# A new order for the instructions of a fused Mamba and mixture-of-experts kernel, in the same four slots

## What is computed

```
x = x + 0.5 * ffn(layernorm(x))      # 8 experts 128 -> 512 -> 128, the top 2 weighted
h = layernorm(x)
x1 = h + mamba(rmsnorm(h))           # in_proj, conv of 4 taps, silu, x_proj, dt_proj, softplus,
                                     #   a scan over t with 16 states, gate, out_proj
m  = mamba(rmsnorm(x1))
x = x + x1 + memory_attend(m)        # m + 0.1 * (masked m m^T v) W_read
x = x + 0.5 * ffn(layernorm(x))
```

## Time and profile before

| | |
|---|---|
| median of 3 runs | 1785.68 us (1783.99 to 1789.38) |
| the profiled execution | 1783.98 us, of which the span 1782.2 us |
| VectorE | 1580.4 us busy, 89% of the span |
| TensorE | 1455.7 us busy, 82% |
| ScalarE | 1102.2 us busy, 62% |
| GpSimd | 300.9 us busy, 17% |
| DMA | 131.93 MB, mostly the 224 additions of `G` into `acc` |
| tensor clock, mean | 0.908 of 2.4 GHz |

### The profile page before, as it was taken

The page is one execution under the profiler, slowest core; times in us unless marked ns, Lnnn a source line. Parts: engine busy times, 40 slices in busy tenths (PEclk is TensorE's granted clock), DMA queues, the critical chain, the costliest instruction groups (busy, mean ns, idle before and its releaser), DMA issues. The chain is left out here.

```text
span 1782.2 us, 26252 instructions
## 1 busy us (share of the span) xinstructions
PE 1455.7 (82%) x8672; PEld 1251.2 (70%) x8672; DVE 1580.4 (89%) x2421; ACT 1102.2 (62%) x2173; POOL 300.9 (17%) x366
## 2 busy tenths in 40 slices
PE   5878656888989888988989888988989888568768
PEld 4767545777778777777878677776878677357757
DVE  5259999999999999999999999999999999999821
ACT  2267455756767666756766667756776677447422
POOL 0001121122112211122112221122112121121100
PEclk9989767999999899998999899998999899669869
DMA  5014344443443334433443334433344344443400
GB/s 200 1 23 79 76 80 82 89 83 60 78 85 73 66 73 88 89 72 60 82 86 72 72 72 90 85 75 61 73 79 80 63 81 89 83 83 72 93 8 7
DMA packets 43947, 131.93 MB, mean 74 GB/s; under 512 B 3984, under 2 KB 12176, under 8 KB 43664
## 3 DMA queue, kind: packets, MB, share of 16 engines
q0 software_dynamic: 32256, 117.45, 34.7%
q1 hardware_dynamic: 11536, 12.56, 2.2%
HBM read 10.46 MB, written 2.10 MB: 7 GB/s over the span
## 5 line engine op out<-in xcount | busy, mean ns | idle before, releaser
L927 DVE TENSOR_TENSOR_SCAN hs<-dA,dbu 128x1024 f32<-128x1024 f32 x256 | 583.8, 2286 | 5.2 <-issue 3.6
L575 ACT ACTIVATE raw<-b_h 128x512 f32<-128x512 f32 x512 | 305.7, 598 | 323.1 <-PE b_h L327 308.6
L636 ACT ACTIVATE dA<-delta,A 128x255 f32<-128x255 f32 x1024 | 421.7, 495 | 13.2 <-DVE delta L900 6.8
L1118 POOL DMA_DIRECT2D acc<-G x224 | 195.5, 873 | 1101.2 <-DVE G L939 658.0
L404 PE MATMUL b_r<-bcr,selr 128*128 128x256 f32 x1024 | 240.2, 330 | 134.2 <-DVE G L939 74.3
L917 DVE TENSOR_TENSOR dbu<-du,b_r 128x1024 f32<-128x1024 f32 x256 | 306.0, 1206 | 5.4 <-issue 3.6
L325 PE MATMUL b_h<-xh,w1h 128*128 128x512 f32 x512 | 245.5, 479 | 78.0 <-DVE ob L853 31.3
L404 PEld LDWEIGHTS b_r<-bcr,selr 128*128 128x128 f32 x1024 | 174.8, 203 | 175.2 <-DVE G L939 82.2
L939 DVE TENSOR_TENSOR G<-hs,b_r 128x1024 f32<-128x1024 f32 x224 | 271.9, 1214 | 8.2 <-issue 5.4
L334 PE MATMUL b_out<-w2s,raw 128*128 128x128 f32 x2048 | 252.3, 275 | 0.0
L334 PE MATMUL b_h<-w2s,raw 128*128 128x128 f32 x2048 | 250.2, 275 | 0.0
(11 more groups left out here) (137 smaller groups left out, 1408.2 us busy)
## 6 DMA issues: line engine op xcount, KB each, us to landing
acc<-G POOLq DMA_DIRECT2D x224, 512.0 KB, 4.5
xin<-x_dram SPq DMA_DIRECT2D x8, 256.0 KB, 2.8
raw<-w_dram SPq DMA_DIRECT2D x1, 2048.0 KB, 11.0
out_dram<-ob SPq DMA_DIRECT2D x8, 256.0 KB, 2.8
prm<-pack_dram SPq DMA_DIRECT2D x1, 1124.5 KB, 5.2
hs<-sel_dram SPq DMA_DIRECT2D x2, 512.0 KB, 12.3
G<-sel_dram SPq DMA_DIRECT2D x2, 512.0 KB, 7.5
dA<-early_dram SPq DMA_DIRECT2D x1, 512.0 KB, 11.4
```

Of the source, the lines that this page charges most:

```text
L575: do(hT[e % 2][:, c, :], H[i % 2][:, :], ACT.Silu).then_inc(f_hact, 1)
L636: last = do(dA[j % 4][:, d, k, 1:], delta[b][:, k, 1:], ACT.Exp, scale=A[:, k, s:s + 1])
L927: V.tensor_tensor_scan(flat(hs[j % 2]), flat(dA[j % 4]), flat(dbu[j % 2]), 0.0, ALU.mult, ALU.add)\
L1118: Q.dma_start(acc[b][:, :, :, :].rearrange("p d h t -> p (d h t)"), G[j % NG][:, :, :, :].rearrange("p d h t -> p (d h t)"), accum_op=ALU. ...
```

## The change: what it does

`ORDER` is written anew for all four slots on all four engines. The helpers, their instructions, operands, buffers and waits stay; no word moves to another slot. The numbers behind `p` change too, so that the experts' pieces stand elsewhere between the spreads. Two texts of the table (slot 2) as they were and as they are:

```diff
 "vector":
-        "flow b0 flog b1 s0 g0 gate s1 ftop xsum b2 g1 un lx s2 b3 g2 fweights s3 f0 b4 b5 ln g3 s4 f1 b6 g4 low "
-        "s5 s6 g5 b7 unx g6 s7 delta g7",
+        "b0 flow s0 flog ftop b1 g0 b2 gate s1 xsum g1 b3 fweights un s2 s3 g2 lx f0 b4 g3 s4 b5 f1 g4 ln low s5 "
+        "b6 b7 g5 unx s6 s7 g6 g7 delta",
```

More of the change, by code:

```diff
@@ L46 @@
     "tensor": (
[8 rows of a table removed]
+        "t0 t1 t2 fturn in fgate t3 p1 t4 t5 p8 t6 p1 xp t7 t8 p4 dt p3 t9 m1 t10 t11 p5 t12 m2 t13 p1 t14 p2 t15 "
+        "m3 m4 p3",
+        "t0 p2 t1 p1 t2 p1 t3 p4 t4 p2 t5 p2 out p4 t6 t7 p3 turn t8 p2 t9 in t10 p1 t11 p4 t12 p4 t13 p1 t14 p2 "
+        "xp t15 p1 dt p2",
+        "t0 fturn t1 fgate p1 t2 t3 p4 t4 p1 t5 out p3 t6 p4 turn t7 t8 in t9 p3 t10 xp t11 p3 t12 p2 t13 p2 dt "
+        "p1 t14 p2 t15 p5",
+        "t0 t1 turng t2 p2 in t3 p2 t4 p5 t5 p1 t6 p2 t7 xp t8 p3 t9 p1 t10 dt m1 p2 m2 t11 p2 t12 p2 t13 p7 t14 "
+        "p2 m3 t15 p2 m4",
     ),
     "scalar": (
[4 rows of a table removed]
[4 rows of a table added]
     ),
     "vector": (
[1 row of a table removed]
[1 row of a table added]
         "g5 s6 b7 g6 s7 xb g7",
[6 rows of a table removed]
[6 rows of a table added]
     ),
```

## The result

| | before | after |
|---|---|---|
| median of the runs | 1785.68 us | 1797.04 us (5 runs, 1795.43 to 1799.98) |
| ratio, 95% interval | | 1.0068 [1.0056, 1.008] |
| span of the profiled execution | 1782.2 us | 1795.2 us |
| mean tensor clock | 0.908 | 0.904 |
| VectorE, from its first scan product to the start of its last `gate` | 1584.3 us | 1600.6 us |

The last two rows are worked out from VectorE's timeline and its busy time: 111.14 to 1695.44 us and 109.37 to 1710.00 us for the first, 111.14 to 1689.18 and 109.37 to 1704.20 for the second, which is the prediction's 53.7 us but for its ends. The 16.3 us that the long part grew are the loss; the set-up ahead of it was 1.8 us shorter and the end 1.5 us, and 16.3 - 1.8 - 1.5 is the 13.0 us of the span. These are of one execution each.

A forecast was written before the change was run, and what follows sets the result against it. VectorE was taken to set the pace, with 53.7 us not busy. Gains of 17.5 us less new waits of 2.1 and 1.4 made 14.0, so 1783.98 became 1770.0, a median of 1771.7 us; 8-in-10 range 1763 to 1789.

The forecast's parts named there:

- Slot 2's logits: Slot 2: a scan as cover ends VectorE's wait on TensorE's logits; 6.9 us gained, nearly all waits on logits.
- `gate`: Slots 0, 1 and 2: `gate` stands behind two or more further words, so its 2.1 us of waits go.
- `xsum`: VectorE's three waits on `xsum` for `out`, 2.3 us, taken as gone, with a reserve for new waits.
- the 1.4 taken: Slot 2's `xsum`: less cover, margin 0.6 us; new waits of 0.2 us in 7 groups, bad case 15 us.
- the third tight place: Slot 0's `mask` waits for `m2`, now behind 22 pieces and not 18; taken as 0, upper bound 9 us.
- 17.5 - 1.3 - 1.4: Gross gain 17.5 us, less slot 0's logits wait in group 1 counted as gone, less slot 2's new `xsum` waits.
- The pairs: Slots 1 and 2: scans or products right behind the one they read, set apart; 0.61 us x 8 groups = 4.9 us.
- First, slot 0's logits: Slot 0: only low part and one product as cover; new waits 7 x 0.3 = 2.1 us, upper end 19 us.
- The set-up and the end: Ends outside VectorE's long stretch keep their order but for a few words; left at zero.
- the table switches of ScalarE: ScalarE: table switches stay 18 a group.
- (c): One tight place gives the gain back: slot 0's logits 1788.7 us or slot 2's `xsum` 1785.3 us; chance 0.21.
- (d): Slower: TensorE at 1.2 GHz at slot 0's logits and slot 2's `xsum`; +16.5, 1802 us; chance 0.12.

The follow-up runs named there:

- 6: Changed kernel with slot 3's old texts back on all engines: 1777.99 us; separately, kernel before with the new VectorE text in slot 0 alone: 1822.63 us.
- 7: Changed kernel, loops kept, `rs` ahead of `a1` in slot 1 and slot 3's tail (`mask`, `v`, `m3`, `m4`) done earlier: 1768.33 us.
- 1: TensorE's loop over groups 1 to 5 written out: in the changed kernel 1768.4 us, in the kernel before 1788.2 us.

## Why the prediction was wrong, point by point

**Slot 2's logits (6.9 us), `gate`: right; `xsum` half.** No wait of slot 2 on the logits is left (6.3 us in seven waits; the other 0.6 of the 6.9 stood in slot 0 of group 6, at 1314.9 us), and `gate`'s row is gone. `x` has 1.6 us against the 1.4 taken, and that is luck: the 1.4 stood for new waits in slot 2 of seven groups, which are 0.13 us at most, and the 1.6 are two of the three old waits, in groups 0 and 7, that were counted as gone. The same holds for the third tight place: `mask` in slot 0 waits at most 0.16 us. The balance of the long part leaves 18.8 us of gain outside slot 0's logits (25.3 + 2.2 + 6.4 + 1.2 of new cost, below, less the 16.3 measured); the prediction had 17.5 - 1.3 - 1.4 = 14.8. The difference was not followed up; it is made of idles too small to have rows.

**The pairs (4.9 us): right in kind.** Measured alone in the kernel before they gave 3.6 us; from scan to scan in slot 1 it was 0.48 us, where 0.43 were predicted. What the Trainium skill has measured (VectorE: DVE Perf Modes, The DRAIN you can't avoid) is eight copies, which take as long with a semaphore after each as with one after the last. Carried over to a scan or product that reads what stood just before it, it would make the pairs free, and here that doesn't hold.

**"First, slot 0's logits": the step that failed.** The prediction took "0.3 us, near the full-clock row, since the new list keeps TensorE busier just before: 7 x 0.3 = 2.1 us; upper end 19 us". In the three groups that begin without a turn the waits were 1.5, 0.18 and 0.10 us, and without TensorE's loop 2.0 us over seven groups against the 2.1 taken: there the sum was right, though as a mean of many zeros and one 1.3. Where the clock was low without a turn (groups 1 and 6 in 6 and 7) it was 1.6 to 2.6, near the 2.7 of the upper bound. At the four turns they were 4.8 to 7.0. Two errors are in it. The bound: I took its upper end from group 1, which enters the loop and has no turn before it, and priced the turn itself by the 1.00 us that stands in VectorE's, so nothing in the sum stood for an instruction list that is not there. And the sign of the argument: that TensorE is busier just before the turn was taken as good for the clock, and it is what exposes the fetch. TensorE had 2.50 us of slack ahead of its first spread, and in it the fetches went unseen. The row that could have told me was in the trace of before: a stop marked issue between two matmuls of `in`, 0.22 and 0.29 us at two of the turns: a fetch that came almost in time.

**What was not in the sum at all.** The turn shows on VectorE a second time, ahead of `b0`: 7.2 us against 5.0 over groups 1 to 6, so 2.2 more. The scan beside `rs`: 6.4 us. Slot 2's `f1` in group 7: 1.2 us. The set-up and the end, left at zero, gave 3.3 us, of which at least 0.7 is chance: the same set-up took 0.7 us more in the version without TensorE's loop. And the table switches of ScalarE, said to stay 18 a group, went from 19 to 18 in the loop's group; no term rests on them.

**The bill.** Predicted change of the profiled execution -14.0, measured +13.0, so 27.0 us to explain: slot 0's logits 27.5 - 2.2 (those of before) against 2.1 - 1.3 in the sum, 24.5; the turn at `b0` 2.2; the scan 6.4; `f1` 1.2; the ends -3.3; the further small gains -4.0. That is 27.0. The small gains are the remainder, so that it closes proves nothing; the run without TensorE's loop is what shows the first two terms, and the one with `rs` ahead the third.

**The rivals.** (c) named the right place with 2.7 us a group, and the outcome lies beyond it. (d) gave 1802 us and the right sign, by TensorE at 1.2 GHz. The clock took part but did not begin it. The windows of the kernel after, before and behind the second stop of the turn into group 4 (the last three figures are clock, DMA share and GB/s):

```profile
903.00:914.00 11.00, 4.76 (x32) 4.28 (x32) 9.48 (x18) 7.22 (x16) 0.86 (x1) 0.81 0.61 124
914.00:923.00 9.00, 8.06 (x32) 6.92 (x32) 2.12 (x4) 2.42 (x4) 0.00 (x0) 0.66 0.00 1
```

TensorE is busy 4.76 of 11 us, and then runs `in` at a mean granted clock of 0.66: from the matmul behind the stop to the last of the logits it takes 922.70 - 914.94 = 7.76 us, where the kernel with slot 3 of before takes 907.07 - 901.76 = 5.31. So some 2.5 us of this turn's wait are the low clock, which here follows the stops; without them, in that kernel, the same stretch runs at 1.00. It can come without a stop too, and then costs 1.3 to 2.8 us (group 4 in 1, groups 1 and 6 in 6, groups 1, 5 and 6 in 7), so (d)'s mechanism is real at a third of the wait's size. And (d)'s other place, slot 2's `xsum`, did not wait.

**What would show it.** Named were "a new row with seven or more waits on `lg` (slot 0)" for wrong altogether, and it came, with five; and an idle that falls "from 53.7 to about 40 us" for right. Without the loop it is 40.0.

**What stays open.** What exactly asks for a fetch, and when, the records don't show: they have its start and its size. That q8 feeds TensorE is read from the count that changes with its loop alone. From the start of a fetch to the instruction behind the stop 2.3 to 2.9 us pass at the four turns of the kernel after, while the transfer itself has 0.9 to 1.3 us; the rest has no record. And why TensorE's clock is low in some groups and executions under the thin cover, and not in others, was not tested.

## What to carry to other kernels

An order that is better inside the loop's body can be worse at its turn: look at the back-edge as a place of its own, find the engine that has its last work done with 2 to 3 us to spare there, and keep that slack, or write the loop out. A stop marked issue between two matmuls of one line near a turn was a fetch that only just arrived each time it was seen here, down to 0.22 us. And price a place by a row of the same kind: a first pass through a loop says nothing of the others.

## What the runs showed of the hardware

A turn of TensorE's loop takes two fetches of 16 KB here, each 2.3 to 2.9 us from its start to the instruction. At the turn into group 4 TensorE stood 3.90 + 3.28 us, and VectorE 8.4 us (1.52 + 6.88), some 2.5 of them the low clock behind the stops. With a transfer of 512 KB ahead of the fetches the four turns cost 28.6 us, with additions of 128 KB 8.0. The Trainium skill has the parts of this: instruction memory is refilled in blocks of 16 KiB (Runtime: NRT & Kernel Launch, Terms), and one such line holds 256 instructions (Advanced Engine Details and Errata, ISA Cache); the trace agrees with the size. The latter page's Control Flow Timing gives a branch some 0.05 to 0.1 us; no row here shows the branch by itself, and the stops behind it were 3.90 and 3.28 us.

A GpSimd operation (`rs`, 0.72 us beside a product, 1.03 us here) that starts 0.10 us ahead of a scan makes it 0.80 us longer. The same operation behind the scan's start costs the scan nothing (2.28 us) and takes 2.18 us itself.
